# Twenty unread matmuls between the second pair's turns and the first value product, in bodies of four tiles

## The chip, the cores and the metric

The kernel runs on one core of a Trainium2 chip. The metric is the device time of one execution in microseconds (us), as the median of several runs. Each engine (TensorE, VectorE, ScalarE, GpSimd, SyncE) works through its own queue in order and waits on semaphores for the others.

## What is computed

1250 rows of 512 features go through a graph layer (a mean over 20000 edges, two products, a normalisation over the rows, added to the input) and then through a mixture of four experts. Each row goes to its two best experts, and each expert is a transformer layer over its own rows:

```
h = _ln(xf, ln1_w, ln1_b)
qkv = h @ ipw.T + ipb
q, k, v = jnp.split(qkv, 3, axis=-1)
...
scores = jnp.where(mask[None, None, :], scores, NEG)
a = jax.nn.softmax(scores, axis=-1)
o = jnp.einsum('hts,hsd->htd', a, v).transpose(1, 0, 2).reshape(T, E)
o = o @ opw.T + opb
x1 = xf + o
h2 = _ln(x1, ln2_w, ln2_b)
m = jax.nn.gelu(h2 @ w1.T + b1, approximate=False) @ w2.T + b2
return x1 + m
```

T is the number of rows, E = 512, H = 8 heads of 64, the hidden width is 256. The results of an expert are weighted and added to its rows.

## The kernel before, in words

The graph layer and the choice of experts fill the first 400 us. Then every engine runs a loop over the four experts. The rows of an expert are collected into tiles of 128, and the number of tiles is known only at run time. So each engine's program holds five bodies (`ARMS`, L91), one for each allowed split of tiles, and at the head of each expert it reads a number and branches to the body that fits (`chosen`, L119 to L142). `Shape.short` (L114) is true for bodies of four tiles. In the run shown, the experts take four, four, ten and four tiles.

A value in 32 bits is multiplied as two halves in 16 bits, high and low. `product` (L1396) makes three passes (high by high, low by high, high by low) over four chunks of 128 features, so 12 matmuls for each 128x512 result. `w16` holds the expert's weights as two halves: ScalarE casts the high one (L852), GpSimd makes the low one (L583) and counts it in `s_elo`.

The start of a body, where the change lies:

- ScalarE scales the rows of the first four tiles (`first_rows`, L984, tile `probs_t` by the profile's names).
- TensorE turns them, a pair of tiles at a time: `turn_first(p)` (L1417) waits for the scaled rows, and does 16 transposes in two groups of 8 (`turn`, L1405; the transposes are at L1409). The second pair's groups wait until ScalarE has emptied the banks (`s_affine`).
- ScalarE applies scale and bias (`scaled_columns`, L948 to L958, tile `t`), and VectorE splits the result into the halves `hT` (`split_columns`, L2077 to L2084; L2082 and L2083) and counts in `s_hsplit`.
- `value(0)` (L1424) waits for the weights (`s_elo`, L1617) and for the first pair's `hT`, and makes the values of tile 0, 12 matmuls at L1401. ScalarE copies them out (L989).
- In a body of four tiles TensorE then makes the query and key projections of the first two heads, `side_of(0, 0)` and `side_of(0, 1)` (L1623 and L1624; the matmuls are at L1522), which need the `hT` of all tiles; ScalarE and VectorE split them (L1067, L1069, L2196 to L2200). `side_of(0, 1)` waits for ScalarE's copy of the first one. Then come the other values, the scores of the first head and the loop over the eight heads (`short_head`, L1580).
- In a longer body the other turns come first, then the projections for 512 columns at a time.

The order of each queue is written out by hand. Unread matmuls stand in the program already: between the last head and the output projection (L1679 and L1680), 18 in a body of four tiles and 32 in a longer one. They write the two banks `sbk`, which hold scores and, later, output projections, and which nobody reads at that point.

VectorE's first work in a body is to copy the expert's parameters (`ep`, L2102 and L2103). After it comes the splitting of `hT`.

Of the kernel before, what the change touches and what calls it, by code (L numbers as in the profile page):

```python
# [53 lines left out]
NPB = 4  # L54
SHORT = 512
LOW = 32
WARM_SHORT, WARM_LONG = 18, 32
UP = 5
AHEAD = 4
SPARE = 2  # L60
# [100 lines left out]
def program(nc, x, src, dst, gnn_w, gnn_par, gate_w, gate_b, ew, epar_d, erow, out):  # L161
    stack = ExitStack()
    with stack:
# [3 lines left out]
        def sb(name, shape, dt, where=None):  # L167
            return (where or stack).enter_context(nc.sbuf_tensor(name, shape, dt))
# [71 lines left out]
        w16 = sb("w16", [P, 2, WCOLS], F16)  # L240
        ident_h = sb("ident_h", [P, P], F16)
# [82 lines left out]
        pp, sbk, stb, pvb = banks[0:2], banks[2:4], banks[4:6], banks[6:8]  # L324
# [866 lines left out]
        def _(pe):  # L1191
# [13 lines left out]
            for c in range(KC):  # L1205
                last = nc.tensor.matmul(banks[5][:, 0:NE], mean_d[:, :], gate_t[:, c, :], start=(c == 0),
                                        stop=(c == KC - 1))
# [108 lines left out]
            for t in range(NT):  # L1316
                mine = slice(t * TT, (t + 1) * TT)
                for k, a in enumerate((xnT_hi, xnT_lo)):
                    for c in range(KC):
                        last = nc.tensor.matmul(banks[6][0:TT, t * 2 * NE:(t + 1) * 2 * NE], a[:, c, mine],  # L1320
                                                gate_16[:, c, :, :].rearrange("p k e -> p (k e)"),
                                                start=(k == 0 and c == 0), stop=(k == 1 and c == KC - 1))
# [82 lines left out]
            def turn(p, q):  # L1405
                for i in range(2):
                    c = 2 * q + i
                    for k in range(2):
                        last = nc.tensor.transpose(pp[q][:, (2 * i + k) * P:(2 * i + k + 1) * P],  # L1409
                                                   normal[:, (2 * p + k) % 4, c * P:(c + 1) * P], ident[:, :])  # L1410
                last.then_inc(s_turned, 1)

            def expert_pe(e, shape):
# [3 lines left out]
                def turn_first(p):  # L1417
                    pe.wait_ge(s_n1, normed1.at(2 * p + 2))
                    for q in range(2):
                        if p > 0:  # L1420
                            pe.wait_ge(s_affine, affine.at(2 * p + q - 1))
                        turn(p, q)

                def value(t):  # L1424
                    pe.wait_ge(s_hsplit, hsplit.at(2 * (t // 2) + 2))
                    if t >= 2:
                        pe.wait_ge(s_vcopy, vcopied.at(t - 1))
                    product(stb[t % 2][:, :], lambda a, c: hT[a][:, c, t * P:(t + 1) * P],
                            lambda b, c: w16[:, b, c * 3 * D + 2 * D:(c + 1) * 3 * D], KC).then_inc(s_v, 1)
# [184 lines left out]

                turn_first(0)
                turn_first(1)
                pe.wait_ge(s_elo, e * NWP + QKV_P)  # L1617
                value(0)
                if shape.short:
# [134 lines left out]
            for e, shape in chosen(nc, nc.tensor, "pe", arms):  # L1754
                expert_pe(e, shape)
# [713 lines left out]
```

## Time and profile before

| | us |
|---|---|
| median of three runs | 1287.71 |
| lowest and highest of the three | 1287.62, 1289.76 |
| the profiled execution | 1292.2 |
| its span, first to last instruction | 1290.4 |
| mean granted TensorE clock in it | 0.906 of full speed |

The rows further down are of that one profiled execution, with times in us from the start of its span. A timeline row has the start, the length, the engine, the line, the operation, the tile written and the tiles read, the shapes, and the number of instructions merged. In brackets stands how long the engine was idle before it and what ended that. Names such as `bank`, `t` or `probs_t` are the program's, with buffer numbers left out.

### The profile page before, as it was taken

The page shows a single profiled execution, that of the slowest core. Times are in us where ns is not written, and L with a number is a line of the kernel's source. Part 1 is how long each engine was busy: PE and PEld are TensorE (multiplying, and loading weights), DVE is VectorE, ACT ScalarE, POOL GpSimd, SP SyncE. Part 2 cuts the span into 40 slices and gives each one's busy share as a digit, 9 for nine tenths or more (in the row PEclk, how much of TensorE's full clock was granted, in tenths as well). Part 3 has the DMA queues.
Part 4 walks back from the last instruction along what each step waited for, and adds up shares of the span by engine and source line. Part 5 has one row for each costly group of instructions (what it writes and reads, how often), then busy time and mean ns, then how long its engine had stood idle before and what let it go on. Part 6 is the DMA issues. An engine that isn't in the chain of part 4 may idle for free.

```text
span 1290.4 us, 19562 instructions
## 1 busy us (share of the span) xinstructions
PE 1050.3 (81%) x5170; PEld 581.3 (45%) x5171; DVE 731.5 (57%) x1604; ACT 453.8 (35%) x843; POOL 329.3 (26%) x305
## 2 busy tenths in 40 slices
PE   1986789998943887867886989989798899979984
PEld 1654467777831343433443434434343335433332
DVE  5485635442371478636775565656748347745753
ACT  1301112221322465335626234434344442235521
POOL 3102233442745534214331030000000123203311
PEclk9987799998655988989888989999999899989997
DMA  5192000000436424111323020000002112110010
GB/s 152 46 276 88 2 2 0 0 0 1 145 104 192 130 66 164 44 66 49 115 88 123 1 66 1 1 0 0 0 0 82 50 39 71 56 58 1 1 32 34
DMA packets 36270, 75.63 MB, mean 59 GB/s; under 512 B 9644, under 2 KB 9942, under 8 KB 35915
## 3 DMA queue, kind: packets, MB, share of 16 engines
q1 hardware_dynamic: 27563, 55.91, 14.0%
q0 software_dynamic: 8320, 16.49, 4.4%
q10 hardware_dynamic: 288, 2.10, 0.5%
q8 instruction: 40, 0.66, 0.2%
q14 instruction: 59, 0.48, 0.1%
HBM read 49.06 MB, written 26.70 MB: 59 GB/s over the span
## 4 chain that ended last, share of the span: by engine, by line
PE 64%; DVE 14%; issue 9%; ACT 6%; DMA 3%; POOL 2%; SPq 1%; DVEq 1%; ACTq 0%; POOLq 0%
PE bank L1401 16%; PE bank L1492 9%; PE bank L1260 8%; PE bank L1299 5%; PE bank L1522 4%; PE bank L1577 3%; DVE den L2238 2%; PE bank L1295 2%; PE bank L1456 2%; PE bank L1477 2%; PE bank L1479 2%; PE bank L1226 2%; DMA table<-rows 1%; PE bank L1536 1%; PE bank L1561 1%
## 5 line engine op out<-in xcount | busy, mean ns | idle before, releaser
L1854 DVE TENSOR_SCALAR oh_src<-iota,edge 125x1250 f16 x178 | 101.5, 570 | 105.5 <-PE bank L1260 99.9
L1492 PE MATMUL bank<-probs_t,v_head 128*128 128x512 f32 (+1 forms) x288 | 147.0, 594 | 7.0 <-ACT probs_t L1044 6.4
L1044 ACT ACTIVATE probs_t<-bank 128x512 f32<-128x512 f32 x144 | 81.5, 573 | 135.9 <-PE bank L1479 135.3
L2151 DVE TENSOR_REDUCE mx<-bank 128x1 f32<-128x512 f32 x144 | 88.5, 657 | 63.8 <-PE bank L1456 62.9
L583 POOL TENSOR_TENSOR w<-w_stage,w 128x1024 f16<-128x1024 f32 x40 | 86.1, 2166 | 139.2 <-ACT w L852 139.2
L1260 PE MATMUL bank<-oh_src,oh_dst 125*125 x534 | 110.8, 357 | 2.8 <-issue 0.6
L1577 PE MATMUL bank<-probs_t,v_head 128*128 128x128 f32 (+2 forms) x192 | 88.7, 549 | 5.8 <-ACT probs_t L1095 4.3
L1401 PE MATMUL bank<-hT,w 128*128 128x256 f16 (+1 forms) x552 | 89.3, 325 | 1.4 <-DVE hT L2083 1.4
L1260 PEld LDWEIGHTS bank<-oh_src,oh_dst 125*125 x534 | 70.1, 142 | 43.7 <-issue 24.4
L1522 PE MATMUL bank<-hT,w 128*128 128x512 f16 x288 | 73.2, 387 | 7.8 <-ACT t L1069 7.8
L1401 PE MATMUL bank<-w,hT 128*128 128x512 f16 x264 | 67.5, 410 | 9.2 <-DVE hT L2083 9.2
L1401 PEld LDWEIGHTS bank<-hT,w 128*128 128x128 f16 (+1 forms) x552 | 56.8, 103 | 32.9 <-issue 2.8
L2224 DVE TENSOR_REDUCE mx<-bank 128x1 f32<-128x128 f32 (+2 forms) x96 | 48.9, 551 | 40.0 <-PE bank L1536 39.7
L1095 ACT ACTIVATE probs_t<-bank 128x128 f32<-128x128 f32 (+2 forms) x96 | 44.8, 488 | 72.9 <-PE bank L1563 72.3
L1492 PEld LDWEIGHTS bank<-probs_t,v_head 128*128 128x128 f32 x288 | 53.1, 195 | 29.5 <-ACT probs_t L1044 14.7
L1401 PE MATMUL bank<-w,oT 128*128 128x512 f16 x264 | 64.2, 395 | 0.0
L730 POOL COPY v_head<-x_in 128x640 f32 x6 | 4.3, 724 | 223.2 <-PE bank L1492 223.2
L956 ACT ACTIVATE t<-bank,ep 128x256 f32<-128x256 f32 x44 | 21.3, 564 | 109.4 <-PE bank L1702 109.4
L1456 PE MATMUL bank<-k_hi,q_hi 66*128 66x512 f16 x144 | 43.9, 382 | 18.8 <-DVE mx L2151 10.8
L1477 PE MATMUL bank<-q_hi,k_hi 97*128 97x512 f16 x144 | 54.8, 381 | 2.7 <-ACT q_hi L1022 2.7
L873 ACT COPY a_row<-bank 125x512 f32<-125x512 f32 (+1 forms) x30 | 13.3, 515 | 117.6 <-PE bank L1273 117.6
L1479 PE MATMUL bank<-q_both,k_both 128*128 128x512 f16 x144 | 54.4, 377 | 0.0
(316 smaller groups left out, 1951.0 us busy)
## 6 DMA issues: line engine op xcount, KB each, us to landing
w_stage<-in_ew_dram SPq DMA_DIRECT2D x40, 512.0 KB, 4.4
lists<-zeros SPq DMA_DIRECT2D x1, 10340.0 KB
x_in<-lists SPq DMA_DIRECT2D x15, 517.0 KB, 5.2
x_mem<-lists SPq DMA_DIRECT2D x3, 1024.0 KB, 5.2
x_mem<-lists SPq DMA_DIRECT2D x1, 2560.0 KB, 10.1
table<-rows SPq DMA_DIRECT2D x10, 251.0 KB
out_dram<-x_mem SPq DMA_DIRECT2D x10, 250.0 KB
big<-in_x_dram SPq DMA_DIRECT2D x10, 224.0 KB
```

The lines of the kernel that those rows point to most:

```text
L583: nc.gpsimd.tensor_tensor(w16[:, 1, cols], w_stage[:, p % WB, :], w16[:, 0, cols], ALU.subtract).then_inc(s_elo, 1)
L1044: nc.scalar.activation(probs_t[:, x % NPB, 0:cn], stb[x % 2][:, 0:cn], ACT.Exp).then_inc(s_exp, 1)
L1260: last = nc.tensor.matmul(ab[k][0:TT, 0:cn], oh_dst[:, bass.ds(slot, 1), i, :], oh_src[:, bass.ds(slot, 1), i, c0:c0 + cn], start=False, s ...
L1401: last = nc.tensor.matmul(bank, lhs(a, c), rhs(b, c), start=(n == 0 and c == 0 and bias is None), stop=(n == 2 and c == chunks - 1))
L1456: nc.tensor.matmul(sbk[i % 2][:, 0:cn], q_hi[0:MARK + 2, hd, t * P:(t + 1) * P], k_hi[0:MARK + 2, hd, c0:c0 + cn], start=True, stop=True). ...
L1477: nc.tensor.matmul(stb[i % 2][:, 0:cn], k_hi[0:SHIFT + 1, hd, kt * P:(kt + 1) * P], q_hi[0:SHIFT + 1, hd, c0:c0 + cn], start=True, stop=False)
L1479: nc.tensor.matmul(stb[i % 2][:, 0:cn], k_both[:, hd, kt * P:(kt + 1) * P], q_both[:, hd, c0:c0 + cn], start=False, stop=True).then_inc(s_ ...
L1492: nc.tensor.matmul(pvb[(hd * nq + s) % 2][:, 0:cn], v_head[:, hd, kt, :], probs_t[:, (hd * nx + i) % NPB, 0:cn], start=(k == 0), stop=(k = ...
L1522: last = nc.tensor.matmul(pp[0][:, 0:nt * P], w16[:, a, c0:c0 + P], hT[b][:, c, 0:nt * P], start=k == 0, stop=k == 3 * KC - 1)
L1577: nc.tensor.matmul(pvb[(hd * nq + s) % 2][:, 0:cn], v_head[:, hd, j % 2 * nt + kt, :], probs_t[:, i, 0:cn], start=(k == 0), stop=(k == nk ...
L1854: nc.vector.tensor_scalar(oh_src[:, bass.ds(slot, 1), i, 0:N].rearrange("p a n -> p (a n)"), iota[:, :], edge[:, 0, i, bass.ds(g, 1)], Non ...
L2151: nc.vector.tensor_reduce(mx[:, hd, t, s:s + 1], sbk[i % 2][:, 0:cn], AX.X, ALU.max).then_inc(s_mx, 1)
```

## The change

```diff
@@ -54,7 +54,7 @@
 NPB = 4
 SHORT = 512
 LOW = 32
-WARM_SHORT, WARM_LONG = 18, 32
+WARM_SHORT, WARM_LONG, WARM_FIRST = 18, 32, 20
 UP = 5
 AHEAD = 4
 SPARE = 2
@@ -1614,6 +1614,9 @@
 
                 turn_first(0)
                 turn_first(1)
+                if shape.short:
+                    for k in range(WARM_FIRST):
+                        nc.tensor.matmul(sbk[k % 2][:, :], ident_h[:, :], w16[:, 0, 0:512], start=True, stop=True)
                 pe.wait_ge(s_elo, e * NWP + QKV_P)
                 value(0)
                 if shape.short:
```

In bodies of four tiles TensorE makes 20 matmuls of 128x512 after the second pair's turns. The stationary operand is the identity in 16 bits, the moving one 512 columns of the high weights, and the two banks `sbk` are written in turn. They wait for no semaphore and count in none, and their results are not read.

## Rows read from the trace of the kernel before

**Rows 1.** The page's first part: busy time and share of each engine.
```profile
PE 1050.3 (81%) x5170; PEld 581.3 (45%) x5171; DVE 731.5 (57%) x1604; ACT 453.8 (35%) x843; POOL 329.3 (26%) x305
```
**Rows 2.** Timeline of TensorE, start of the first body of four tiles (A).
```profile
410.87 2.03 PE L1409 MATMUL bank<-ident,probs_t 128*128 128x128 f32 x8 [3.33 <-ACT t L956]
413.42 4.34 PE L1401 MATMUL bank<-w,hT 128*128 128x512 f16 x12 [0.53 <-DVE hT L2083]
417.59 2.75 PE L1522 MATMUL bank<-hT,w 128*128 128x512 f16 x12
421.79 2.76 PE L1522 MATMUL bank<-hT,w 128*128 128x512 f16 x12 [1.44 <-ACT t L1069]
```
**Rows 3.** The same, start of the second body of four tiles (B).
```profile
550.11 0.66 PE L1409 MATMUL bank<-ident,probs_t 128*128 128x128 f32 x4 [0.26 <-ACT t L956]
556.81 4.32 PE L1401 MATMUL bank<-w,hT 128*128 128x512 f16 x12 [6.04 <-DVE hT L2083]
560.97 2.75 PE L1522 MATMUL bank<-hT,w 128*128 128x512 f16 x12
```
**Rows 4.** The same, start of the fourth body, four tiles (C).
```profile
1135.88 2.03 PE L1409 MATMUL bank<-ident,probs_t 128*128 128x128 f32 x8 [0.34 <-ACT t L956]
1139.04 5.04 PE L1401 MATMUL bank<-w,hT 128*128 128x512 f16 x12 [1.13 <-DVE hT L2083]
1143.91 2.75 PE L1522 MATMUL bank<-hT,w 128*128 128x512 f16 x12
```
**Rows 5.** The chain of work that ended last, at B: start, length, engine, line.
```profile
556.81 4.32 PE bank L1401 x12
561.13 2.60 PE bank L1522 x12
```
**Rows 6.** Windows: length, busy of PE, PEld, DVE, ACT, POOL; clock, DMA share, GB/s.
```profile
413.42:416.57 3.15, 3.15 (x8) 1.18 (x9) 2.86 (x4) 1.00 (x2) 2.54 (x3) 0.50 0.78 192
550.77:553.17 2.40, 0.00 (x0) 0.00 (x0) 0.00 (x0) 0.00 (x0) 0.00 (x0) 1.00 0.29 110
556.81:559.99 3.18, 3.18 (x8) 1.18 (x9) 2.12 (x4) 0.99 (x2) 0.00 (x0) 0.50 0.85 339
1133.47:1139.04 5.57, 3.99 (x17) 3.00 (x17) 2.53 (x7) 2.98 (x7) 0.00 (x0) 0.50 0.31 65
1139.04:1143.68 4.64, 4.64 (x11) 1.63 (x12) 2.12 (x4) 1.00 (x2) 0.00 (x0) 0.50 0.48 181
```
**Rows 7.** The unread matmuls of before: their line, and TensorE's timeline in the first body.
```profile
L1680 PE MATMUL bank<-hT,ident_h x86: 379/379/380, 508.8 to 1238.8; 128*128 128x512 f16 x86
508.82 4.05 PE L1680 MATMUL bank<-hT,ident_h 128*128 128x512 f16 x18
513.40 0.38 PE L1398 MATMUL bank<-bias_rows,ones_k 33*128 33x512 f16 x1 [0.53 <-DVE oT L2241]
513.72 2.76 PE L1401 MATMUL bank<-w,oT 128*128 128x512 f16 x12
```
**Rows 8.** Weight loads of the value product at B, two neighbours.
```profile
557.63 0.15 PEld L1401 LDWEIGHTS bank<-w,hT 128*128 128x128 f16 x1 [0.28 <-issue]
558.06 0.15 PEld L1401 LDWEIGHTS bank<-w,hT 128*128 128x128 f16 x1 [0.28 <-issue]
```
**Rows 9.** Timeline of VectorE at the start of B.
```profile
553.82 0.18 DVE L2102 COPY ep<-epar 128x30 f32 x1 [5.38 <-issue]
...
558.30 0.69 DVE L2083 TENSOR_TENSOR hT<-t,hT 128x512 f16<-128x512 f32 x1
```
**Rows 10.** Timeline of TensorE in the fourth body, unread matmuls and output projection.
```profile
1235.13 4.05 PE L1680 MATMUL bank<-hT,ident_h 128*128 128x512 f16 x18
1242.22 0.38 PE L1398 MATMUL bank<-bias_rows,ones_k 33*128 33x512 f16 x1 [3.04 <-DVE oT L2241]
1242.53 4.45 PE L1401 MATMUL bank<-w,oT 128*128 128x512 f16 x12
```
**Rows 11.** Windows, as rows 6: a low stretch in the first body.
```profile
469.15:474.60 5.45, 5.45 (x14) 2.42 (x15) 2.66 (x6) 1.01 (x3) 1.98 (x4) 0.50 0.05 20
```

## The prediction, made before the changed kernel ran

> **What bounds the kernel now.** I first read the page's head: TensorE is busy 81% of the span, with no other engine above 57%, so time on TensorE's own queue is likely to be time of the kernel [rows 1]. The share says nothing about one stage, so I went to the stretch that the diff touches, the start of an expert's body. The kernel has four such starts, one for each expert. The third expert's body has ten tiles and does not take the new branch, so the new matmuls run three times, 60 in all. I call the three places, the starts of the first, second and fourth body, A, B and C.
>
> TensorE's timeline shows how much idle time lies between the last turn and the first value product (12 matmuls of 128x512): 0.53 us at A, 6.04 us at B, 1.13 us at C, each ended by VectorE's hT at L2083 [rows 2, 3, 4]. The reader is to see that the hole is large only at B. After the value product the first side product (L1522) follows at once in all three, and the chain of work that ended last, shown for B, runs through both [rows 2 to 5]. So what lengthens or shortens this stretch of TensorE's queue moves everything behind it.
>
> The windows then show the granted clock. At A the clock is at its lower level (0.50, 1.2 GHz) until 416.57, and at the upper one (1.00, 2.4 GHz) after. At B it is at the upper level still for 2.40 us of idling behind the turns, but at the lower one when the value product starts, until 559.99. At C it is low from 1133.47, just before the turns, to 1143.68 [rows 6]. From the start of the value product the low time is 3.15, 3.18 and 4.64 us. What it costs follows from the starts: 12 matmuls take 413.42 to 417.59 = 4.17 us at A, 4.16 at B and 4.87 at C [rows 2, 3, 4]. At the upper level 18 unread matmuls of the same shape take 4.05 us, the last one 0.379 of it, so (4.05 - 0.379) / 17 = 0.216 us each [rows 7]; 12 make 2.59. The excess is 1.58, 1.57 and 2.28 us, which is 0.5 us for each us of low time. That agrees with the lower level's spacing of 0.43 us, read from its weight loads [rows 8].
>
> **The change part by part.** It removes and moves nothing, adds no wait, no semaphore and no DMA. It adds 20 matmuls and their 20 weight loads on TensorE, behind turn_first(1) and ahead of the wait for the weights. Loads cost nothing of their own: they last 0.10 to 0.15 us and lie beside a running matmul, as in the rows of the existing unread ones [rows 7, 8]. They write the banks sbk, which nobody reads until the first scores, so nothing else waits for them; behind them on TensorE are the value product and all that follows.
>
> Work added, at the upper clock: 20 x 0.216 = 4.32 us a body. The Trainium skill, "TensorE: Matmul & The Clock Gate", section "Back-to-back issue gap", gives about 131 ns for each 512-column matmul in a stream of weight loads and matmuls; by it the 20 would be 2.6 us and the sum below 3.4 us lower. The rows of this very instruction say 0.216 us, so the measurement decides.
>
> At B: the turns end at 550.77, the 20 can run at once at the clock that the turns had, and end near 550.6 + 4.48 = 555.1 (18 in 4.05, two more at 0.216). The value product is not ready before VectorE's hT at 556.8, and that chain has nothing of TensorE's after the turns (VectorE starts its body's first operation at 553.82, after 5.38 us with no releaser but its own queue) [rows 9]. So the cost is nothing; cover left over is 1.7 us, and without it each missing us would be paid in full. The gain: with the clock kept up, the value product takes 2.6 us and not 4.2. The next gate is the second half of hT, ready at 558.99 (558.30 + 0.69) [rows 9], and the shorter value product ends after it, near 559.6, so the whole gain passes on. It is 1.6 us by B's own low time; by the mean of the three, (3.15 + 3.18 + 4.64) / 3 = 3.66 us, it is 0.5 x 3.66 = 1.8 us. Bounds: 0 (the clock falls all the same) and 2.3 (a low time as at C).
>
> At A and C the cover is the idle time plus the 0.15 us or so by which a following matmul starts before the end of the one ahead (417.59 against 417.76): 0.7 us at A and 1.3 at C. The rest of the 4.32 us is on the path: 3.6 and 3.0 us. Can it come back through the clock? The clock is low when the 20 begin. If low time after the beginning of the dense stream is as long as it was before, only other matmuls bear it, and nothing comes back. That is what I take. Bounds: if the clock rises at the very instants of this profile, the low time is longer by the cover, and half of that comes on top (A 4.0, C 3.7). If it rises 1.5 us sooner (the distance between the rows' 3.15 and 4.64) it is 0.7 less (A 2.9, C 2.3). The turns might count towards the rise. At C they kept TensorE busy for 3.99 of 5.57 us and the clock stayed at 0.50 [rows 6]. The same page, section "Part 4: PE-mode transpose", says that transposes do not count as busy in the same way; by that rule too they bring no early rise, and the trace agrees.
>
> Sum: A +3.6, B -1.8, C +3.0 = **+4.8 us**. With each place's clock exactly as profiled it is 4.0 - 1.6 + 3.7 = +6.1. The profiled execution took 1292.2 us (span 1290.4 and 1.8 around it), so it would take 1297.0; the median of the three runs shown is 4.5 us lower, at 1287.7, and there I get 1292.5 us. A measurement of this kernel can tell about 0.2% (2.6 us) from no change, and +4.8 is 0.37%.
>
> **The rivals.**
> *The clock falls at B all the same.* A gap of 1.7 us is left behind the 20. For it: in the fourth body 18 unread matmuls, a gap of 3.04 us, and then 12 matmuls in 4.45 us, at the lower level [rows 10]. Against it: after the same 18 and a gap of 0.53 us the clock was up [rows 7], and at A it survives 1.44 us ahead of the second L1522 product, which takes 2.76 us, the length at the upper level [rows 2]. 1.7 is nearer to these. Price: the gain is lost, +6.6, or 1294.3 us. Chance 12%.
> *Within 0.2%.* The new matmuls bring the rise early at A and C and B is the dear case: 2.9 + 2.3 - 2.3 = +2.9 at the bounds above, and if A and C run ahead by one more such step of 0.7 us each, +1.5, or 1289.2 us. Decisive is whether the low time from the first new matmul is under 3 us; no row shows one so short. Chance 11%.
> *Faster.* Later low stretches vanish. At 469 us a wait for k_both leaves TensorE idle, and the following 5.45 us run at 0.50, a cost of 2.7 us [rows 11]. A displaced queue meets the clock otherwise, and such a stretch may be gone. From +4.8 to below -2.6 it needs three of them gone at 2.7 (then -3.3, or 1284.4 us) and none new. The waits that cause them are on VectorE and the same as before, so as many should come as go. Chance 4%.
> *The change doesn't do what it says,* as the 20 could be covered everywhere: excluded at A and C, where the value product's operand was there 0.7 and 1.3 us after the turns. Chance 1%, time as before.
>
> **How the numbers follow.** My forecast, with A and C paying about three quarters of the added work and B gaining, has 72%. Slower by over 0.2%: 72 + 12 less 3 for a forecast that lands under the line = 81%. Within: 11 + 1 + 3 = 15%. Faster: 4%. The range: the sum's low bounds give +2.9 and its high ones 4.0 + 3.7 - 0 = +7.7; the three runs themselves are 2.1 us apart. I take 1290.2 to 1295.4.
>
> **What would show it.** Right: 60 matmuls of the new line; at A and C they start at once behind the turns, mostly 0.43 us apart, last some 6 us, and the value product behind them takes 2.8 us, ending 3 to 4 us later than before counted from the turns; at B they last about 4.5 us, then a gap of 1.5 to 2 us, and the value product takes 2.8 us at clock 1.00, starting no later. From the value product's end on, the bodies have the lengths they had, but for single low stretches. Wrong: a value product at B of over 4 us; new matmuls at A or C mostly 0.216 us apart from their first; a body that is shorter behind its first side product by more than a low stretch explains.

## The result, and the profile after

| | before | changed |
|---|---|---|
| median of 5 runs each | 1288.64 us | 1296.66 us |
| lowest and highest | 1287.62, 1293.52 | 1292.35, 1297.80 |
| profiled execution, and its span | 1292.2, 1290.4 | 1292.35, 1290.6 |

The ratio is 1.0043, with an interval of 1.0024 to 1.0061: the change makes the kernel slower, by some 5.5 us. The two medians lie further apart, by 8.0 us, but each comes from five runs that scatter by over 5 us, so I go by the ratio and its interval. The two profiled executions differ by 0.2 us only, and that of the changed kernel is its fastest run. One pair of profiles would have hidden the loss; the experiments below have the same kernels in more executions.

TensorE's part of the page's list of busy times, after:

```profile
PE 1060.7 (82%) x5230; PEld 587.0 (45%) x5231; DVE 730.3 (57%) x1604; ACT 453.4 (35%) x843; POOL 328.7 (25%) x305
```

There are 60 matmuls and 60 weight loads more than in [rows 1], and no other engine has an instruction more. The timeline of TensorE at the three starts (A, B and C in the prediction) after the change:

```profile
410.44 2.03 PE L1409 MATMUL bank<-ident,probs_t 128*128 128x128 f32 x8 [2.20 <-ACT t L956]
412.26 5.01 PE L1619 MATMUL bank<-w,ident_h 128*128 128x512 f16 x20
417.11 2.75 PE L1401 MATMUL bank<-w,hT 128*128 128x512 f16 x12
419.70 2.75 PE L1522 MATMUL bank<-hT,w 128*128 128x512 f16 x12
...
550.34 0.66 PE L1409 MATMUL bank<-ident,probs_t 128*128 128x128 f32 x4 [0.25 <-ACT t L956]
550.83 4.48 PE L1619 MATMUL bank<-w,ident_h 128*128 128x512 f16 x20
557.02 2.76 PE L1401 MATMUL bank<-w,hT 128*128 128x512 f16 x12 [1.71 <-DVE hT L2086]
559.62 2.75 PE L1522 MATMUL bank<-hT,w 128*128 128x512 f16 x12
...
1132.96 2.03 PE L1409 MATMUL bank<-ident,probs_t 128*128 128x128 f32 x8 [0.34 <-ACT t L956]
1134.78 5.56 PE L1619 MATMUL bank<-w,ident_h 128*128 128x512 f16 x20
1140.17 2.75 PE L1401 MATMUL bank<-w,hT 128*128 128x512 f16 x12
1142.76 2.75 PE L1522 MATMUL bank<-hT,w 128*128 128x512 f16 x12
```

The measure that I use for a start is the time from the end of the last turn to the first L1522 matmul, because the turns end when ScalarE lets them, and everything behind that matmul waits in the same queue. At A it was 417.59 - 412.90 = 4.69 us [rows 2] and is 419.70 - 412.47 = 7.23. At B it was 10.20 [rows 3] and is 8.62. At C it was 6.00 [rows 4] and is 7.77. The windows show the clock that the new matmuls met (columns as in [rows 6]):

```profile
412.26:413.40 1.14, 1.14 (x4) 0.46 (x3) 1.01 (x3) 1.14 (x3) 0.83 (x2) 0.53 0.52 129
550.83:555.31 4.48, 4.48 (x22) 1.86 (x19) 0.88 (x4) 0.00 (x0) 0.00 (x0) 1.00 0.26 66
555.31:557.02 1.71, 0.00 (x1) 0.01 (x1) 1.65 (x4) 1.04 (x3) 0.00 (x0) 1.00 0.73 259
557.02:559.62 2.60, 2.60 (x12) 1.18 (x13) 2.11 (x4) 0.99 (x2) 0.00 (x0) 1.00 1.01 397
1134.78:1137.00 2.22, 2.22 (x7) 0.85 (x6) 2.13 (x5) 1.89 (x4) 0.00 (x0) 0.51 0.87 320
```

B is as forecast to a tenth of a us: 4.48 us of unread matmuls, 1.71 of idling, and the value product at the upper level, against 0.50 in [rows 6]. At A and C the clock came up 1.1 and 2.2 us after the first new matmul. In the profile before it came up 3.15, 3.18 and 4.64 us after the value product began [rows 6]. VectorE's chain at B is not touched. It starts its body 5.36 us after its last work (5.38 in [rows 9]):

```profile
554.04 0.18 DVE L2105 COPY ep<-epar 128x30 f32 x1 [5.36 <-issue]
```

### The profile page after: what moved, and what is told of

The parts are those of the page before. It is cut to its first block, busy times and chain, and to the rows that moved or that the text cites. A ratio compares the mean times of both kernels' runs of the same rounds, so it can differ in the third digit from the quotient of the medians.

```text
span 1290.6 us, 19682 instructions
## 1 busy us (share of the span) xinstructions
PE 1060.7 (82%) x5230; PEld 587.0 (45%) x5231; DVE 730.3 (57%) x1604; ACT 453.4 (35%) x843; POOL 328.7 (25%) x305
## 4 chain that ended last, share of the span: by engine, by line
PE 64%; DVE 14%; issue 9%; ACT 5%; DMA 3%; POOL 2%; SPq 1%; DVEq 1%; ACTq 0%; POOLq 0%
PE bank L1401 15%; PE bank L1492 9%; PE bank L1260 8%; PE bank L1299 5%; PE bank L1522 4%; PE bank L1577 3%; DVE den L2241 3%; PE bank L1295 2%; PE bank L1456 2%; PE bank L1477 2%; PE bank L1479 2%; PE bank L1226 2%; DMA table<-rows 1%; PE bank L1536 1%; DVE oT L2243 1%
## 5 line engine op out<-in xcount | busy, mean ns | idle before, releaser
L1577 PE MATMUL bank<-probs_t,v_head 128*128 128x128 f32 (+2 forms) x192 | 89.6, 554 | 6.7 <-ACT probs_t L1095 5.0
L1522 PE MATMUL bank<-hT,w 128*128 128x512 f16 x288 | 72.5, 385 | 7.8 <-ACT t L1069 7.8
L1401 PE MATMUL bank<-w,hT 128*128 128x512 f16 x264 | 62.3, 387 | 3.0 <-DVE hT L2086 3.0
L1456 PE MATMUL bank<-k_hi,q_hi 66*128 66x512 f16 x144 | 43.0, 375 | 16.0 <-DVE mx L2154 10.6
```

Source lines behind the costliest of these rows:

```text
L1401: last = nc.tensor.matmul(bank, lhs(a, c), rhs(b, c), start=(n == 0 and c == 0 and bias is None), stop=(n == 2 and c == chunks - 1))
L1456: nc.tensor.matmul(sbk[i % 2][:, 0:cn], q_hi[0:MARK + 2, hd, t * P:(t + 1) * P], k_hi[0:MARK + 2, hd, c0:c0 + cn], start=True, stop=True). ...
L1522: last = nc.tensor.matmul(pp[0][:, 0:nt * P], w16[:, a, c0:c0 + P], hT[b][:, c, 0:nt * P], start=k == 0, stop=k == 3 * KC - 1)
L1577: nc.tensor.matmul(pvb[(hd * nq + s) % 2][:, 0:cn], v_head[:, hd, j % 2 * nt + kt, :], probs_t[:, i, 0:cn], start=(k == 0), stop=(k == nk ...
```

## The experiments

There are eleven experiments (three of them repeat a kernel), each run beside the kernel before on the same chip, in three sessions. "Start" is the measure above, from one profile of each kernel. "Body" is the time from the first turn of a body to the first turn of the next (from the last one to the end of the span).

| kernel | ratio and interval | start A, B, C | body 1, 2, 3, 4 |
|---|---|---|---|
| before (profile above) | | 4.69, 10.20, 6.00 | 141.8, 144.3, 441.9, 156.8 |
| before_again | 0.9999, 0.9983 to 1.0014 | 4.16, 10.19, 5.67 | 140.9, 144.0, 439.2, 156.7 |
| changed (profile above) | 1.0043, 1.0024 to 1.0061 | 7.23, 8.62, 7.77 | 141.4, 143.9, 439.1, 159.9 |
| after_again | 1.0024, 1.0007 to 1.0041 | 8.31, 8.62, 7.84 | 143.8, 143.8, 439.1, 160.2 |
| only_fourth | 1.0027, 1.0008 to 1.0045 | 3.76, 10.02, 7.84 | 141.2, 143.9, 442.2, 160.0 |
| only_first_two | 1.0014, 0.9996 to 1.0031 | 8.84, 8.63, 5.77 | 145.2, 143.2, 439.4, 156.7 |
| second_body | 0.9988, 0.9973 to 1.0003 | 5.27, 8.64, 5.77 | 139.0, 143.6, 442.0, 156.5 |
| second_body_again | 0.9986, 0.9968 to 1.0003 | 5.02, 8.64, 5.84 | 141.8, 143.4, 439.4, 156.9 |
| one_column | 1.0001, 0.9983 to 1.0020 | 4.91, 11.14, 5.81 | 138.5, 146.2, 439.4, 156.3 |
| ten | 1.0003, 0.9990 to 1.0016 | 6.49, 11.11, 5.69 | 138.3, 146.2, 439.4, 156.5 |
| thirty | 1.0076, 1.0047 to 1.0106 | 10.77, 8.89, 9.51 | 146.3, 143.9, 446.0, 160.5 |
| forty | 1.0125, 1.0100 to 1.0150 | 12.83, 11.06, 12.12 | 147.2, 146.9, 439.3, 164.7 |
| turns | 1.0040, 1.0026 to 1.0053 | 8.55, 8.62, 7.88 | 144.3, 143.4, 439.3, 160.6 |

The theories of the expectations: the *path theory* is the prediction's. By the *early-rise theory* the new matmuls and the turns bring the clock up sooner, and the loss is smaller. By the *code theory* it is the 40 added instructions that cost, in the stream and at the switches between bodies. The *give-back theory* came up after the first session: what a start gains or loses is changed again further behind, because low clock stretches come, go or change their length there.

**before_again** is the kernel before, with no edit.

> The kernel before, unchanged, against itself: it tells how far the times of one kernel scatter, and where. All theories: ratio 1.000, with single times from about 1287.5 to 1293.5 us as so far. At the starts of the first, second and fourth body the last turn's end and the start of the first side product lie 4.7, 10.2 and 6.0 us apart in the one profile at hand; with another meeting of the clock each may be up to 1 us off (low times of 3 to 5 us behind the value product's start), since a us of low time costs 0.5 us.

Measured: ratio 0.9999, and 12 single times from 1287.49 to 1293.56 us. Starts of 4.16, 10.19 and 5.67 us are all within the limits named. So a single time of either kernel says nothing on a change of 5 us.

**after_again** is the changed kernel, with no edit.

> The changed kernel, unchanged. Path theory: the uncovered part of the 20 matmuls is paid at the first and fourth body, the second gains: +3.6 - 1.8 + 3.0 = +4.8 us. Early-rise theory (the turns and the 20 matmuls raise the clock together, as in the profile where the clock rose 1.1 and 2.2 us after the first new matmul): +2.5 - 1.6 + 1.8 = +2.7 us; the larger difference of the medians so far (8 us) is then scatter from low stretches elsewhere. Code theory (40 more instructions in each body of four tiles make the switch between bodies longer): the switches in the profile, so far with 3.6 us of idling without a releaser, are longer than before by a us or more in a second profile too.

Measured: 1.0024, and with 1.0043 above the two intervals share 1.0024 to 1.0041, or 3.1 to 5.3 us. That holds the path theory's +4.8; +2.7 (1.0021) is in this interval only. The switch to the fourth body idles TensorE for 3.44 us ahead of the turns, and for 3.58 us in the first profile of the changed kernel, against 3.18 in the first profile of before and 3.51 in the second. The difference is under half a us, so nothing speaks for the code theory.

**only_fourth and only_first_two** split the change by the place.

```diff
-                if shape.short:
+                if shape.short and nq == 1:
                     for k in range(WARM_FIRST):
```

> The 20 matmuls only in the body of the fourth expert. Path theory: +3.0 us (+0.23%). Early-rise theory: +1.8 us. Code theory: as the path theory or more. All: the fourth body's last turn's end to first side product takes 7.8 to 9 us in place of 6.0, the starts of the first and second body are as before (4.7 and 10.2 us).

```diff
-                if shape.short:
+                if shape.short and nq > 1:
                     for k in range(WARM_FIRST):
```

> The 20 matmuls only in the bodies of the first two experts. Path theory: +3.6 - 1.8 = +1.8 us (+0.14%). Early-rise theory: +2.5 - 1.6 = +0.9 us. If a displaced queue as such costs (low stretches that come behind the first displacement), it shows here in the bodies behind: over +4 us. The fourth body's start is as before (6.0 us).

Measured: +0.27% (3.5 us) for C alone and +0.14% (1.8 us) for A and B, where the path theory had 3.0 and 1.8. The second interval (0.9996 to 1.0031) still holds no change at all. The two add up to 5.3 us, where after_again had 3.1 us against the same runs of before; each of these figures is uncertain by some 2.3 us. But the fourth body's timeline in only_fourth shows the start only 1.8 to 2.2 us longer than the 5.67 to 6.00 without:

```profile
1135.03 2.03 PE L1409 MATMUL bank<-ident,probs_t 128*128 128x128 f32 x8 [0.34 <-ACT t L956]
1136.85 5.63 PE L1619 MATMUL bank<-w,ident_h 128*128 128x512 f16 x20
1142.31 2.75 PE L1401 MATMUL bank<-w,hT 128*128 128x512 f16 x12
1144.90 2.75 PE L1522 MATMUL bank<-hT,w 128*128 128x512 f16 x12
```

The whole body is 3.3 us longer (160.0 against 156.7). The rest is found 67 to 68 us into the body: counted from the first turn, the matmul that ends a wait for k_both there comes 2.2 us later in only_fourth than in before_again (66.9 against 64.7 us), and the next matmuls of the same line, behind a low stretch, 3.7 us later (71.0 against 67.3). The wait is there in both kernels. Timeline of the kernel before, then timeline and window of the changed one:

```profile
1198.59 0.60 PE L1536 MATMUL bank<-k_hi,q_hi 66*128 66x512 f16 x2 [2.00 <-DVE k_both L2200]
1199.03 1.03 PE L1522 MATMUL bank<-hT,w 128*128 128x512 f16 x4
```

```profile
1197.43 0.60 PE L1536 MATMUL bank<-k_hi,q_hi 66*128 66x512 f16 x2 [1.99 <-DVE k_both L2203]
1197.87 1.40 PE L1522 MATMUL bank<-hT,w 128*128 128x512 f16 x4
...
1198.39:1201.80 3.41, 3.41 (x8) 1.29 (x7) 1.38 (x3) 0.00 (x0) 1.05 (x3) 0.50 0.00 0
```

The same wait of 2.0 us is followed by the upper clock in the one and by 3.4 us of the lower in the other. By the price of 0.5 us that is 1.7 us, and by the body's length less the start's it is 1.3. All three profiles with 20 at C have it, and none of those without. A cost of displacement as such (over 4 us for A and B) did not come: the ratio stands for 1.8 us, and its interval ends at 4.0.

**second_body, second_body_again** keep the matmuls only where the hole is.

```diff
-                if shape.short:
-                    for k in range(WARM_FIRST):
-                        nc.tensor.matmul(sbk[k % 2][:, :], ident_h[:, :], w16[:, 0, 0:512], start=True, stop=True)
+                if shape.short and nq > 1:
+                    with nc.tensor.If(e > 0):
+                        for k in range(WARM_FIRST):
+                            nc.tensor.matmul(sbk[k % 2][:, :], ident_h[:, :], w16[:, 0, 0:512], start=True, stop=True)
```

> The 20 matmuls only where the body of the first two experts is entered for the second expert (a branch at run time, the only place with a hole in TensorE's queue). Path theory: the gain of the start stays whole: -1.5 to -1.8 us (-0.13%). Give-back theory (the time saved is partly paid again by low clock stretches further behind, as body lengths of the profiles so far hint: start 1.5 us shorter, body only 0.5 to 0.9 shorter): -0.5 us. Branch: it may itself cost TensorE up to a few tenths of a us, or a switch like those of 3.5 us if it breaks the instruction stream; then the first body's start shows a gap behind the turns. Second body: last turn's end to first side product 8.6 us (10.1 without). First and fourth as before: 3.8 to 4.7 and 5.7 to 6.0.

> The 20 matmuls in the second expert's body alone, once more, since the first time (ratio 0.9988, 0.9973 to 1.0003) left open whether there is a gain. Path theory: -1.5 us at the start of the second body, whole: 0.9988. Give-back theory: -0.5 us: 0.9996. The second body again takes 143.2 to 143.9 us in the profile, against 143.9 to 144.3 without, and its start 8.6 against 10.0 to 10.2.

Measured: 0.9988 and 0.9986, each with an interval that ends at 1.0003. The start is what both theories said (8.64 and 8.64 us). The second body takes 143.6 and 143.4 us, that is 0.3 to 0.9 less than the 143.9 to 144.3 of the three profiles in which neither A nor B is edited, so part of the 1.5 us is paid again behind. The traces show where: at another wait for k_both, 80 us into the second body. Timeline and window of before_again, then of second_body:

```profile
629.46 0.45 PE L1536 MATMUL bank<-k_hi,q_hi 66*128 66x128 f16 x2 [2.52 <-DVE k_both L2200]
631.10:634.51 3.41, 3.28 (x10) 1.59 (x10) 2.20 (x11) 1.84 (x5) 0.00 (x0) 0.50 0.00 0
...
626.91 0.61 PE L1536 MATMUL bank<-k_hi,q_hi 66*128 66x128 f16 x2 [2.53 <-DVE k_both L2204]
625.80:632.63 6.83, 5.72 (x15) 2.76 (x16) 4.82 (x17) 1.63 (x5) 2.49 (x4) 0.50 0.00 0
```

Counted from the body's first turn, the matmul that ends this wait comes 1.50 us earlier in second_body (81.15 against 82.65 us), so the gain of the start is still whole. The low stretch there lasts 6.8 us in place of 3.4, and behind it (632.98 against 634.76) the lead is 0.73 us. All five profiles with the 20 at B have 6.8 us there; of the three without an edit at A or B, two have 3.4 and the first profile of before has 6.8.

The branch at run time did leave a trace: in the first body, where it skips the matmuls, the gap ahead of the value product is 1.03 us, against 0.22 to 0.53 without the branch. The two ratios stand for gains of 1.5 and 1.8 us, the bodies for 0.3 to 0.9; neither interval excludes that there is none, and the medians of the first (1289.76 against 1289.33 for before) don't show it. So a gain of the whole kernel is not shown.

**ten, thirty, forty** change the number.

```diff
-                    for k in range(WARM_FIRST):
+                    for k in range(WARM_FIRST // 2):
...
+                    for k in range(WARM_FIRST * 3 // 2):
...
+                    for k in range(2 * WARM_FIRST):
```

> 10 matmuls in place of 20, in all bodies of four tiles. Path theory: at the upper clock 10 x 0.216 = 2.16 us, less the cover of 0.7 and 1.3: +1.5 and +0.9 us at the first and fourth start; at the second the ten end some 3.9 us before the value product, and the clock falls as before: gain 0. Sum +2.4 us (+0.18%). Early-rise theory: at the fourth body the clock rises about 2.2 us after the first new matmul, so the start takes 6.5 us or less there (5.8 without, 7.8 with 20), sum about +1 us. Give-back theory: the low stretch at about 68 us into the fourth body, there in all three profiles with the 20 and in none without, comes or stays away by where the displaced queue meets the clock, so with 10 it may be absent (fourth body 157 us long) or present (159).

> 30 matmuls in place of 20. Path theory: between 20 and 40: the start of the fourth body 7.8 + 2.2 = 10.0 us, of the second 8.9 (the 30 take 6.6 us, the hole is 6.2), of the first 8 + 2.2 = 10.3; ratio 1.0070 to 1.0085. Give-back theory: the low stretch at 68 us into the fourth body was there with 20 and 40 and absent with 0 and 10; it is absent or present here by where the queue meets the clock: body 160.8 us without it, 162.1 with it.

> 40 matmuls in place of 20. Path theory: 20 more at the upper clock are 4.3 us at the first and fourth start each, and at the second the cover left (1.7 us) is used up, so 2.6 us: +11.3 on the +3 to +5 of the 20, so +14 to +16 us (+1.15%). Second body: last turn's end to first side product 11.2 us. If unread matmuls are cheaper than their records say (0.131 us each), the sum is +6 to +8. Give-back theory: the same at the starts, and single low stretches of 1.7 to 3.4 us come or go behind them. Fourth body: 157 + 2.0 + 4.3 = 163.2 us, and 164.6 with the low stretch at 68 us.

Measured: 1.0003, 1.0076 and 1.0125. Forty cost 16.1 us (interval 12.9 to 19.3), against the 3.1 and 5.5 of twenty, so 10.6 to 13.0 more, where 11.3 were forecast. That rules out 0.131 us a matmul (+6 to +8 in all). At B the 40 run out of cover:

```profile
559.20 8.80 PE L1619 MATMUL bank<-w,ident_h 128*128 128x512 f16 x40
567.83 2.75 PE L1401 MATMUL bank<-w,hT 128*128 128x512 f16 x12
570.42 2.75 PE L1522 MATMUL bank<-hT,w 128*128 128x512 f16 x12
```

so the start is 11.06 us (11.2 expected), and with thirty 8.89 (8.9 expected). At C, thirty has 9.51 us (10.0 expected; the clock rose 1.3 us after the first new matmul), and its body is 3.8 us longer than 156.7, as much as its start (3.7 us): the wait for k_both is there (1.99 us at 1210.34) but no low stretch behind it. Forty has the stretch again, from 1213.50 to 1216.92, and its body is 8.0 us longer with a start 6.3 us longer. So the low stretch doesn't grow with the number of matmuls. That it is a matter of where the same wait meets the clock, as the give-back theory has it, fits these profiles; no run tests it by itself. The clock meets C in the same place each time: in twelve of the thirteen profiles it fell 0.1 to 0.5 us before the turns of the fourth body (thirty is the other).

Ten missed the path theory's +2.4 us (1.0018 lies above its interval); the early-rise theory's +1 us lies in it. At C:

```profile
1131.80 1.97 PE L1409 MATMUL bank<-ident,probs_t 128*128 128x128 f32 x8 [3.42 <-issue]
1134.11 2.02 PE L1409 MATMUL bank<-ident,probs_t 128*128 128x128 f32 x8 [0.34 <-ACT t L956]
1135.93 3.47 PE L1619 MATMUL bank<-w,ident_h 128*128 128x512 f16 x10
1139.23 2.75 PE L1401 MATMUL bank<-w,hT 128*128 128x512 f16 x12
```

Ten matmuls there cost nothing (5.69 against 5.67 to 6.00), since the value product behind them runs wholly at the upper clock. At A, where the hole is smaller, the start is 6.49 us, 1.9 longer than the mean without. At B they save nothing. They end 3.86 us before the value product, the clock falls in between and stays down for the whole product:

```profile
549.39 2.32 PE L1619 MATMUL bank<-w,ident_h 128*128 128x512 f16 x10
555.58 5.30 PE L1401 MATMUL bank<-w,hT 128*128 128x512 f16 x12 [3.86 <-DVE hT L2086]
```

The start is 11.11 us against 10.02 to 10.20. Whether that 1 us is the ten's doing isn't told apart from how the clock happened to meet the body, since one_column, below, has the same. The first body, for its part, is 138.3 us long in spite of its longer start: the low stretch near 470 us of [rows 11] is missing in it. So in this profile low stretches that went away made up for what the matmuls cost at A.

**one_column** leaves the instructions and takes their work.

```diff
-                        nc.tensor.matmul(sbk[k % 2][:, :], ident_h[:, :], w16[:, 0, 0:512], start=True, stop=True)
+                        nc.tensor.matmul(sbk[k % 2][:, 0:1], ident_h[:, :], w16[:, 0, 0:1], start=True, stop=True)
```

> 20 matmuls of one column in place of 512, so the same count of instructions with next to no work. Code theory (the added instructions lengthen the switches or starve TensorE's queue): a loss like that of the full ones, and switches of over 3.6 us at the third and fourth body. Path theory: a matmul of one column takes some 0.05 to 0.09 us from the next, 20 take 1.0 to 1.8 us; less the cover 0.7 and 1.3 that is 0.3 to 1.1 us at the first start and 0 to 0.5 at the fourth, nothing at the second, where the clock falls as before (start 10.1 us). Sum +0.3 to +1.6 us, ratio 1.0003 to 1.0012.

Measured: 1.0001, with an interval that ends at 1.0020 (2.6 us), under the +4.8 of the full ones, and with switches of 3.55 and 3.46 us, like those of the kernel before. The code theory falls: what costs is the matmuls' time. The 20 last 0.72 us (0.03 us from one to the next, where I expected 0.05 to 0.09), and are covered at C:

```profile
1133.19 0.72 PE L1619 MATMUL bank<-w,ident_h 128*128 128x1 f16 x20
1134.44 4.93 PE L1401 MATMUL bank<-w,hT 128*128 128x512 f16 x12 [0.53 <-DVE hT L2086]
```

The value product behind them is as slow as in [rows 4]. It starts 0.53 us after the last of them, and the clock rises 4.43 us after it begins, as late as without new matmuls. The start of B is 11.14 us, with the clock down from 548.4 to 558.6, through the whole value product, and the first body is short, 138.5 us, as with ten.

**turns** puts 40 transposes in the place of the 20 matmuls.

```diff
-                    for k in range(WARM_FIRST):
-                        nc.tensor.matmul(sbk[k % 2][:, :], ident_h[:, :], w16[:, 0, 0:512], start=True, stop=True)
+                    for k in range(2 * WARM_FIRST):
+                        nc.tensor.transpose(sbk[k % 2][:, 0:P], ident[:, :], ident[:, :])
```

> In place of the 20 matmuls 40 transposes of 128x128 of the identity, so the same kind as the turns. It tells whether turns raise the clock. If they do as matmuls do: at the first and fourth start the 40 go from 0.245 us each to 0.13 after some 1 to 3.5 us, last 6 to 7.5 us, and the value product behind them runs at the upper clock (2.6 us). If they don't: they last 9.8 us there, and the value product takes 3.6 to 4.9 us. At the second start they last 5.2 us at the upper clock and the product then takes 2.6 us if turns keep it up, 4.2 if not. Time: +8 us if they raise it (5.2 a body at the upper clock, covers 0.7, 5.8, 1.3, ramps 1 us each), +18 us if not.

Measured: 1.0040, or +5.2 us (interval 3.4 to 6.8), under the 8 of "they raise it" and far from the 18 of "they don't". One part of what is missing from the 8 is that the 40 are shorter than I took them to be: 4.53 us at B, not 5.2. Timeline and windows at C:

```profile
1136.43 5.66 PE L1619 MATMUL bank<-ident 128*128 128x128 f32 x40
1141.93 2.75 PE L1401 MATMUL bank<-w,hT 128*128 128x512 f16 x12
...
1136.43:1138.73 2.30, 2.30 (x12) 2.30 (x12) 2.21 (x5) 2.04 (x4) 0.00 (x0) 0.50 0.86 298
1138.73:1141.93 3.20, 3.20 (x32) 3.19 (x30) 1.14 (x3) 0.00 (x0) 0.00 (x0) 1.00 0.29 106
```

The clock rises in the middle of the transposes, 2.30 us after the first, as with the matmuls (2.2 to 2.3 us at C in three profiles), and at B they keep it up as well (start 8.62). From the clock's fall at 1131.90, just before the turns, to its rise TensorE did nothing but transposes, so the transposes of this kernel raise the clock and hold it, as the matmuls do.

## Why the prediction was right, and where a step was off

The forecast of +4.8 us (1292.5 against a median of 1287.7) stands against ratios of 1.0043 and 1.0024, or 5.5 and 3.1 us. The direction and the cause are shown: the loss goes with the time of the unread matmuls (one_column nothing, forty +16 us), and C alone gives a loss that is clear of noise. The shares of A and B are read from their starts; A and B together (+1.8 us) and B alone (-1.5 and -1.8) are not clear of noise as times of the kernel. That the sum came so near is in part luck, since two terms were off in opposite ways, as the points below show.

- *60 matmuls at 0.216 us.* Right. Sum and single starts fit it, and the Trainium skill's 131 ns of "TensorE: Matmul & The Clock Gate", "Back-to-back issue gap", is not seen: at B the 20 last 4.48 us and the 40 last 8.80, so (8.80 - 4.48) / 20 = 0.216 us.
- *A, +3.6 us.* Right. The starts without new matmuls are 4.69, 4.16, 3.76, 5.27 and 5.02 us, mean 4.58 (the last two with the branch); with 20 they are 7.23, 8.31 and 8.84, mean 8.13: +3.55. The size holds on average only: the clock rose 1.1, 3.3 and 4.3 us after the first new matmul, and 1.9 to 3.3 us after the value product's start without them.
- *B, -1.8 us.* Size a little off. Without, the start takes 10.14 us (mean of 10.20, 10.19, 10.02); with the 20 it is 8.63: -1.5, which is nearer to B's own low time (-1.6) than to the mean of three places that I preferred. And "so the whole gain passes on" failed: the second body is only about 0.5 us shorter (144.1 on average in the three profiles with A and B unedited, 143.6 in the five that have the 20 at B). In second_body some 0.8 us of it went in the low stretch 80 us in.
- *C, +3.0 us.* The term came out near by luck. The step that failed is "if low time after the beginning of the dense stream is as long as it was before". It was 4.6 us behind the value product's start (4.64, 4.59), and 2.2 to 2.3 behind the first new matmul. What differs is that these follow the turns without a hole; one_column, which leaves a hole of 0.53 us and little work, rises as late as before. By my own sum that is 0.5 x 2.4 = 1.2 us less: +1.8, against +2.0 measured (7.82 less 5.80). What filled up the term to 3.3 is the low stretch behind the wait for k_both, which the prediction allowed only as something that comes as often as it goes.
- *"Mostly 0.43 us apart" at A and C.* Off, by the same step: of the 19 distances between the new matmuls 5 are 0.43 us at C (in all three profiles) and 2, 7 and 10 at A; nearly all others are 0.22.
- *"The trace agrees" on the turns.* Wrong. That 4 us of turns among 5.6 us left the clock at 0.50 is true, but it doesn't show that transposes don't count: with 40 of them the clock rose. The sentence of the Trainium skill, "TensorE: Matmul & The Clock Gate", that the full clock does not engage for transpose mode ("Part 4: PE-mode transpose") does not hold for these transposes. Whether they run in that mode the trace doesn't show: at the upper clock they lie 0.108 us apart for 128 columns in 32 bits, as many ns a column as this kernel's other 32-bit matmuls (L1577, 0.43 us for 512).
- *The rival at B* (the clock falls all the same) came with 20 and a gap of 1.7 us in none of five profiles; with ten and a gap of 3.86 us it did.
- *The early-rise rival* was half true: 2.2 to 2.3 us at C, and 1.1, 3.3 and 4.3 at A, in three profiles. It did not bring the change under 0.2% in either ratio, since B gained less as well and the low stretch behind C came on top; but after_again's interval (from 1.0007) does not exclude a value under it.
- *The faster rival* found no support: low stretches moved, and the one that moved for good was a loss.

Sum of the parts as measured by bodies: the first +2.5 (143.5 in three profiles against 140.9 in five, each scattering by 3 to 4 us), the second -0.5, the fourth +3.3 (160.0 against 156.7), so +5.3 us. A late start of the second body is part of the first one's length, and the two together are 287.1 us with the 20 at A and B (three profiles) and 285.4 without (three): +1.7, near the prediction's +1.8. The third body, with no edit, was 439.1 to 439.4 us in nine profiles, 441.9 to 442.2 in three and 446.0 in one, by which low stretches it had, and that is a good part of the scatter of single times. What stays open is why the clock meets the fourth body in the same place in nearly every execution, and whether the 1.5 us at B alone is a gain of the whole kernel.

## What to carry to other kernels

Unread matmuls pay only where a measured hole is longer than they last: 4.5 us in a hole of 6.2 gained 1.5 us at the start of the body, the same in holes of 0.7 and 1.3 us cost 3.6 and 2.0. Follow a gain or a loss to the end of the body: behind later waits of 2.0 and 2.5 us the low stretches changed, by which 0.8 of the 1.5 us was lost again and 1.3 us came on top of the 2.0. Too few of them gain nothing (10 in the long hole left 3.9 us of idling, and the clock fell). If one program text serves several places, measure the hole at each before adding work to all, and take several profiles of each kernel where the expected change is no larger than the scatter of its runs.

## What was not expected of the hardware

- Transposes of 128x128 in 32 bits raise the clock: 2.30 us after the first of 40 at C, like matmuls.
- A matmul of one column follows the one before it after 0.03 us (20 in 0.72 us), though each is recorded as 0.165 us.
- The same wait of 2.0 us, in the same place of the program, is followed by the upper clock in eight profiles and by 3.4 us of the lower in five (all with 20 or 40 matmuls, or 40 transposes, ahead of it), at 1.2 to 1.8 us each (body length less start).
